# Self-attention's keys and queries leave their products turned and are moved to their heads inside SBUF

## What is computed

```python
nq = _rms(x @ w_cq, g_qnorm)                                   # latent, 96 wide
q_nope = (nq @ w_dq_nope).reshape(B, T, 16, 32)
q_rope = _rope((nq @ w_dq_rope).reshape(B, T, 16, 64), cos, sin)
q = concatenate([q_nope, q_rope], -1)
kw = (x @ w_wink).reshape(B, T, 16, 96)                        # window keys
kw = concatenate([kw[..., :32], _rope(kw[..., 32:], cos, sin)], -1)
a1 = _attn(q, k1, v1, causal=True)      # k1 from a 32 wide latent
a2 = _attn(q, ks, vs, causal=False)     # 64 selected tokens
a3 = _attn(q, kw, vw, causal=True)
out = (g0 * a1 + g1 * a2 + g2 * a3) @ w_proj
# _rope: x1 * c - x2 * s, x1 * s + x2 * c on the two halves (32 each) of the 64
```

## Time and profile before

| | us |
|---|---|
| median of 3 runs | 1769.17 (1767.9 to 1771.75) |
| the profiled execution | 1767.97 |
| its span in the trace | 1766.3 |
| PE busy | 1711.8 (97%) |
| DVE busy | 1193.7 (68%) |
| POOL busy | 1038.8 (59%) |
| ACT busy | 877.4 (50%) |

### The profile page before, as it was taken

The page is one execution under the profiler, slowest core; times in us unless marked ns, Lnnn a source line. Parts: engine busy times, 40 slices in busy tenths (PEclk is TensorE's granted clock), DMA queues, the critical chain, the costliest instruction groups (busy, mean ns, idle before and its releaser), DMA issues.

```text
span 1766.3 us, 33699 instructions
## 1 busy us (share of the span) xinstructions
PE 1711.8 (97%) x11512; PEld 1341.5 (76%) x11512; DVE 1193.7 (68%) x3890; ACT 877.4 (50%) x2824; POOL 1038.8 (59%) x1451
## 2 busy tenths in 40 slices
PE   7899999999999999999999789999999999999998
PEld 4676675766766767767657568999999999999997
DVE  4668767767777777687677568565756575657557
ACT  1675856846947848668579552222222222222221
POOL 2455655745736746657557476664856485648553
PEclk9899999999999999999999999999999999999999
DMA  5000000000000000000000110101010101010001
GB/s 179 7 2 8 7 8 7 1 8 7 2 8 7 2 8 8 1 14 2 8 1 2 49 49 25 48 1 48 1 48 1 48 1 49 1 48 1 1 1 48
DMA packets 24667, 33.89 MB, mean 19 GB/s; under 512 B 5104, under 2 KB 20976, under 8 KB 24368
## 3 DMA queue, kind: packets, MB, share of 16 engines
q1 hardware_dynamic: 24496, 31.73, 5.5%
HBM read 29.62 MB, written 2.10 MB: 18 GB/s over the span
## 4 chain that ended last, share of the span: by engine, by line
PE 84%; ACT 7%; DVE 4%; issue 3%; POOL 1%; SPq 0%; DMA 0%; DVEq 0%; POOLq 0%; ACTq 0%
PE ps_S L1423 26%; PE ps_Y L2220 20%; PE ps_H L2220 19%; ACT pr L854 5%; PE ps_O L1423 5%; PE ps_T L1655 5%; PE ps_X L1423 2%; PE ps_T L1489 2%; PE ps_X L1489 2%; PE ps_T L1773 1%; PE ps_S L1773 1%; ACT pr L908 1%; DVE h_hi L2183 1%; DVE sm L1334 0%; ACT rot L737 0%
## 5 line engine op out<-in xcount | busy, mean ns | idle before, releaser
L2054 ACT ACTIVATE h_sb<-ps_H,b_sb 128x512 f32<-128x512 f32 x256 | 176.7, 690 | 506.4 <-PE ps_H L2220 479.8
L2008 POOL TENSOR_TENSOR h_lo<-h_sb,h_hi 128x512 fp32r<-128x512 f32 x256 | 363.4, 1448 | 108.8 <-DVE h_hi L2183 108.8
L645 POOL TENSOR_TENSOR pr<-pr,rden 128x128 f32<-128x128 f32 (+2 forms) x768 | 308.0, 437 | 103.8 <-DVE rden L1215 103.8
L2183 DVE CAST h_hi<-h_sb 128x512 fp32r<-128x512 f32 x256 | 240.2, 956 | 129.7 <-ACT h_sb L2054 129.6
L854 ACT ACTIVATE pr<-sm,nmx 128x128 f32<-128x128 f32 (+2 forms) x768 | 311.7, 412 | 24.5 <-DVE nmx L1226 24.5
L2220 PE MATMUL ps_Y<-w_hi,h_lo 128*128 128x256 f32 x1024 | 286.5, 280 | 0.0
L2220 PE MATMUL ps_Y<-w_hi,h_hi 128*128 128x256 f32 x1024 | 286.5, 280 | 0.0
L2220 PE MATMUL ps_Y<-w_lo,h_hi 128*128 128x256 f32 x1024 | 286.4, 280 | 0.0
L680 POOL TENSOR_TENSOR pr<-pr,rden 128x256 f32<-128x256 f32 x256 | 151.4, 614 | 156.1 <-DVE rden L1215 156.1
L1226 DVE CUSTOM_DVE_ANT_0 sm<-ps_S,cmask 128x128 f32<-128x128 f32 (+2 forms) x768 | 192.8, 308 | 40.5 <-PE ps_S L1423 24.7
L2220 PE MATMUL ps_H<-x_hi,w_hi 128*128 128x512 f32 x512 | 200.4, 391 | 0.0
(11 more groups left out here) (241 smaller groups left out, 3284.3 us busy)
## 6 DMA issues: line engine op xcount, KB each, us to landing
w_raw<-in_W SPq DMA_DIRECT2D x16, 1024.0 KB, 6.2
xin<-in_x SPq DMA_DIRECT2D x8, 256.0 KB, 3.3
cin<-in_ctx SPq DMA_DIRECT2D x8, 256.0 KB, 2.6
w_kw<-in_wink SPq DMA_DIRECT2D x2, 768.0 KB, 6.6
w_ks<-in_selk SPq DMA_DIRECT2D x2, 768.0 KB, 9.9
out<-x SPq DMA_DIRECT2D x3, 512.0 KB, 2.9
b_sb<-in_b SPq DMA_DIRECT2D x1, 1024.0 KB, 4.7
w_qd<-in_dq SPq DMA_DIRECT2D x1, 576.0 KB, 4.8
```

Of the source, the lines that this page charges most:

```text
L645: last = pool.tensor_tensor(p_, p_, rden[:, h % 2, n:n + 1].to_broadcast([P, width]), ALU.mult)
L2008: pool.tensor_tensor(h_lo[:, s % 2, ht, :], h_sb[:, ht % 4, :], h_hi[:, s % 2, ht, :].bitcast(F32), ALU.subtract).then_inc(lo_sb.sem, 1)
L2054: ins = act.activation(h_sb[:, ht % 4, :], pst[plan.bank(f)][:, :], ACT.Relu, bias=b1[:, 2 * i + s // NCH, ht:ht + 1])
L2183: dve.tensor_copy(h_hi[:, s % 2, ht, :], h_sb[:, ht % 4, :]).then_inc(hi_sb.sem, 1)
```

## The change

Keys and queries are now computed with the weights held and all 256 tokens moving (`turned_product`), so that features are in the partitions from the start. A unit is now one half of the heads for all 256 tokens. The columns of `dq` and `wink` are put in another order on the host (`STRIP_HEADS`), so that a part of a unit is a tile of 128 partitions (four strips of 32 features, one head each) x 512 (two heads x 256 tokens); these tiles are `pieces`, in the memory of `rot`. Cosine and sine are loaded once more in turned form (`cs_turned`, 128 x 512, 256 KB), as a fifteenth first weight. Rotation, sums and evacuations work on `pieces`. The 16 groups of transposes per row and the 16 copies out of PSUM are gone for these four units; the selected keys are turned as before. Instead `moves` on SyncE issues transfers from `pieces` to `kT` and `qT`, one for each part and strip: 12, 12, 16 and 16 for the units, 56 a row and 448 in all, each 32 partitions x 2 heads x 256 tokens (64 KB). POOL and ACT wait for the transfers of unit u-2 where they waited for its last turn, and PE waits for all four units before head 0.

```diff
+STRIP_HEADS = [4 * j + b for b in range(4) for j in range(4)]
+STRIPS = P // HD
...
-    for n, name in enumerate((
-            ("kwT", 0, 0), ("kwT", 0, 1), ("kwT", 0, 2), "latT", ("kwT", 0, 3),
-            *(("kwT", 1, g) for g in range(4)), *(("qT", t, g) for t in range(NT) for g in range(4)),
-            ("ksT", 0), ("ksT", 1))):
+    for n, name in enumerate(("latT", ("ksT", 0), ("ksT", 1))):
...
+        cs_turned = sb("cs_turned", [P, 2, T])
...
+        pieces = rot[:, :, :, :].rearrange("p u h d -> p u (h d)").rearrange("p u (s n) -> p u s n", s=4)
...
+        moved = [Signal(sem(f"moved_{u}"), 16 * STRIPS * (3 if u < 2 else 4)) for u in range(4)]
...
+        def landed(eng, u, i):
+
+            eng.wait_ge(moved[u].sem, moved[u].at(i + 1, 0))
...
-        N_FIRST, N_MID, N_LATE = 14, 5, 11
+        N_FIRST, N_MID, N_LATE = 15, 5, 11
...
+            load(cs_turned[:, :, :], w["cs_turned"])
...
+            def move(i, u, part):
+
+                kind, half = UNITS[u]
+                for j in range(STRIPS):
+                    dst = slice(HD * part, HD * part + HD)
+                    heads_ = slice(4 * j + 2 * half, 4 * j + 2 * half + 2)
+                    to = kT[dst, heads_, KEEP:KEEP + T] if kind == "kw" else qT[dst, heads_, :]
+                    sp.dma_start(to, pieces[HD * j:HD * j + HD, u % 2, part, :].rearrange("p (h t) -> p h t", h=2)
+                                 ).then_inc(moved[u].sem, 16)
+
+            def moves(i):
+
+                for u in range(4):
+                    sp.wait_ge(rope_out.sem, rope_out.at(i, 2 * u + 1))
+                    move(i, u, 1)
+                    sp.wait_ge(rope_out.sem, rope_out.at(i, 2 * u + 2))
+                    move(i, u, 2)
+                    sp.wait_ge(plan.free_sem(unit_fill(u, "n")), plan.after(unit_fill(u, "n"), i))
+                    move(i, u, 0)
+                    if u >= 2:
+                        sp.wait_ge(plan.free_sem(unit_fill(u, "c")), plan.after(unit_fill(u, "c"), i))
+                        move(i, u, 3)
+
             def turn(i, load_x):
...
                 load_ctx(i, 1)
+                moves(i + 1)
...
                 def rope_sums(u):
                     rows_, n = unit_rows(u)
                     if u >= 2:
-
-                        pool.wait_ge(plan.full_sem(last_turn(u - 2)), plan.after(last_turn(u - 2), i))
...
+                        landed(pool, u - 2, i)
...
                     if u >= 2:
-
-                        act.wait_ge(plan.full_sem(last_turn(u - 2)), plan.after(last_turn(u - 2), i))
-                    ins = act.copy(rows_[:, :, 0:HD], ps(f)[0:n, :].rearrange("p (h d) -> p h d", h=NH))
+                        landed(act, u - 2, i)
+                    if u < 4:
+                        ins = act.copy(pieces[:, u % 2, 0, :], ps(f)[:, :])
...
-                    evacuate(i, f, rot[:, t, :, QK:P], ps(f)[:, :].rearrange("p (h d) -> p h d", h=NH))
+                    evacuate(i, f, pieces[:, t, 3, :], ps(f)[:, :])
...
+                def turned_product(name, weights, moving):
+
+                    pe.wait_ge(plan.free_sem(name), plan.before(name, i))
+                    for b in range(2):
+                        block_ = slice(P * (2 * name[1] + b), P * (2 * name[1] + b) + P)
+                        for c, (w_, x_) in enumerate(zip(weights, moving)):
+                            last = mm(ps(name)[:, T * b:T * b + T], w_[:, block_], x_, c == 0, c == len(weights) - 1)
+                    last.then_inc(plan.full_sem(name), 1)
+
                 def keys(t, s):
-                    product(i, ("kw", t, "nab"[s]), P, HW, tok(xT, t), [w_kw[:, c, s, :] for c in range(NC)])
+                    turned_product(("kw", t, "nab"[s]), [w_kw[:, c, s, :] for c in range(NC)],
+                                   [xT[:, c, :] for c in range(NC)])
...
                 def queries(t, s):
-                    product(i, ("q", t, "nabc"[s]), P, HW, [latT[0:QL, 0, P * t:P * t + P]], [w_q[:, s, :]])
+                    turned_product(("q", t, "nabc"[s]), [w_q[:, s, :]], [latT[0:QL, 0, :]])
...
                 if h == 0:
 
-                    pe.wait_ge(plan.free_sem(("qT", 1, 3)), plan.after(("qT", 1, 3), i))
-                    pe.wait_ge(plan.free_sem(("qT", 1, 2)), plan.after(("qT", 1, 2), i))
+                    for u in range(4):
+                        landed(pe, u, i)
```

More of the change, by code:

```diff
@@ L401, in attention_stage, with split4, strip_part @@
         cmp2 = sb("cmp2", [P, NT, T])
+        pieces = rot[:, :, :, :].rearrange("p u h d -> p u (h d)").rearrange("p u (s n) -> p u s n", s=4)
+        def split4(row):
+            return row.rearrange("p (b t n) -> p b t n", b=2, t=NT)
+        def strip_part(k):
+            if k < 3:
+                at = NT * T + k * (HW // PR_SLOTS)
+                return pr[:, :, at:at + HW // PR_SLOTS].rearrange("p (b t) n -> p b t n", b=2)
+            return split4(rt3[:, :])
         def rot_part(k, n):
@@ L567, in _ @@
             load_ctx(0, 0)
+            moves(0)
             sp.wait_ge(plan.full_sem("xsel"), plan.after("xsel", 0))
@@ L1427, in _ @@
             stage = pr[0:HD, :, :].rearrange("p a b -> p (a b)")
-            for h in range(NH):
-                last = mm(pst["S0"][0:QL, HD * h:HD * h + HD], stage[:, QL * h:QL * h + QL],
+            for n, h in enumerate(STRIP_HEADS):
+                last = mm(pst["S0"][0:QL, HD * n:HD * n + HD], stage[:, QL * h:QL * h + QL],
                           stage[:, NH * QL + HD * h:NH * QL + HD * h + HD])
@@ L1467, in front, with turn_selected @@
             def front(i):
-                def turn_rows(u, groups):
-                    kind, t = UNITS[u]
-                    rows_, n = unit_rows(u)
-                    if kind == "ks":
-                        pe.wait_ge(sel_nope.sem, sel_nope.at(i, 1))
-                    else:
-                        pe.wait_ge(plan.free_sem(unit_fill(u, "n")), plan.after(unit_fill(u, "n"), i))
-                    if kind == "q":
-                        pe.wait_ge(plan.free_sem(unit_fill(u, "c")), plan.after(unit_fill(u, "c"), i))
-                    pe.wait_ge(rope_out.sem, rope_out.at(i, 2 * u + 2))
-                    width = P if kind == "q" else QK
-                    per = 8 if kind == "ks" else 4
-                    for g in groups:
-                        f = ("ksT", g) if kind == "ks" else (kind + "T", t, g)
+                def turn_selected():
+                    rows_, n = unit_rows(4)
+                    pe.wait_ge(sel_nope.sem, sel_nope.at(i, 1))
+                    pe.wait_ge(rope_out.sem, rope_out.at(i, 10))
+                    for g in range(2):
+                        f = ("ksT", g)
@@ L1485, in turn_rows @@
                         pe.wait_ge(plan.free_sem(f), plan.before(f, i))
-                        if kind == "ks":
-                            pe.sem_inc(s_pass, 1)
-                        for k in range(per):
-                            last = pe.transpose(ps(f)[0:width, n * k:n * k + n], rows_[:, per * g + k, 0:width],
+                        pe.sem_inc(s_pass, 1)
+                        for k in range(8):
+                            last = pe.transpose(ps(f)[0:QK, n * k:n * k + n], rows_[:, 8 * g + k, 0:QK],
```

90 lines of the change are left out of this document (29 added, 61 removed).

## The result

The changed kernel takes 1754.36 us (median of five runs, 1749.06 to 1758.62) against 1769.17 for the kernel before, a ratio of 0.9914 with a 95% interval of 0.9889 to 0.9939. It is faster by 0.9%, 26 us slower than the forecast of 1728, and outside the range of 1711 to 1748. The profiled execution took 1749.06 us, span 1747.0, against 1767.97 and 1766.3 before. Measured again beside some of the experiments, the changed kernel took 1759.10 us (1755.80 to 1764.37, six runs). The runs of each kernel scatter: those five lie 9.6 us apart, six of the changed kernel 8.6, and eleven of the kernel before, beside these six, 10.1.

A forecast was written before the change was run, and what follows sets the result against it. TensorE was taken to bound the kernel. Seven rows -37.1, row 0 -5.4 and the start +1.7 gave -40.8 us: profiled 1767.97 to 1727.2, plus 1.2 to the median, 1728.4, predicted as 1728, range 1711 to 1748.

The forecast's parts named there:

- a rule on transfers: Skill's bandwidth rule for the transfers inside SBUF: 0.95 us for 64 KB, against 0.50 us between loads in the trace.
- Removed on PE: In each row, 16 groups of four transposes at 0.44 us leave TensorE: 7.0 us a row.
- New waits: In each row, three waits of TensorE for DVE and ACT grow: 1.7 us a row together, bounds 0 and 3.5.
- Wait (a): Queries of unit 3, at 406.20 us, wait for the bank that ACT's copy frees: 0.5 us a row.
- Wait (b): The product at 412.83 us and its partner wait for banks read by DVE's rotations: 0.6 us a row.
- Wait (c): The scores pair at 419.45 us waits for an ACT copy of 418.33: 0.6 us a row.
- Row 0: First row, without cover: head 0 at 61.0 us instead of 66.45, set by 32 transfers at 0.50 us; gain 5.4 us.
- the slow rival: SyncE's queue becomes the bound: at 0.95 us a transfer, one after another, +34 us, 1803; chance 0.13.
- The start: Before the first matmul, the added 256 KB table lands later than the other first weights: costs 1.7 us, bounds 0.6 and 2.5.
- Transfers hidden in rows 1 to 7: Before head 0 in rows 1 to 7, the transfers have at least 11 us of slack and cost nothing.
- Turned products at nothing: Keys and queries products in the new form cost nothing extra; bounds 0 and 0.09 us for each of 14 products a row.
- waits take the place of the transposes: Rival: in each row the removed transposes covered the DVE and ACT loop, 3.5 us come back: 1743; chance 0.19.

The follow-up runs named there:

- the kernel with the clock held: The changed kernel plus, in each row, 14 dead transposes where TensorE waits and two small dead matmuls before head 0; 1738.77 us.
- the kernel with the moved product: The kernel with the clock held, with the first product of latent values moved from a later step in place of 8 fillers; 1740.29 us.

## Why the prediction was wrong

**The clock, which no term held.** The whole sum stood on groups at clock 1.00, since the earlier trace rows show 1.00, and I never asked what kept it there. Held by fillers, the changed kernel takes 1738.77 us, inside the range; bare, 1754.36 and 1759.10. The falls cost 15.6 and 20.3 us. That is 0.59 of the first miss, 26.4 us, and 0.65 of the 31.1 by the second measurement, and it is shown: fillers in the idles bring it back without taking away any work or transfer; the same fillers elsewhere do not. The Trainium skill, "TensorE: Matmul & The Clock Gate", section "A second HAM failure mode: psum-queue depth-cycling", describes small idles between groups of matmuls, frequent enough that the clock goes to and fro between its two levels. This trace agrees, on fp32 work: five idles of 0.23 to 0.92 us in 30 us, none of them long, and the clock falls there in some rows and not in others. The prediction weighed a rule on transfers against the trace and should have weighed this one.

**Removed on PE, 7.0 us a row: right.** The line turns only 64-column transposes, 128 of them.

**New waits, 1.7 us a row: too small, 2.6.** A row without a fall gains 4.2 to 4.6 us, 4.4 in the middle, so 7.0 - 4.4 = 2.6 came back. Wait (a), behind ACT's copy, was priced at 0.5 and is 0.52. Wait (b), behind DVE's rotations, was priced at 0.6; it is 0.23 as idle and 2.33 - 1.89 = 0.44 more inside the group at 283.62: 0.67. Wait (c), the scores pair behind ACT's copy, was priced at 0.6 and is 0.92. Not priced were a first queries group stretched from 1.89 to 2.23 (at 271.05), and 0.11 more before head 0. Together 0.52 + 0.67 + 0.92 + 0.34 + 0.11 = 2.56, or 2.4 less the old idle of 0.17 that is gone. Seven rows of 0.9 are the 6 us of this step.

**Row 0, gain of 5.4: wrong, 0.4 came.** The mechanism was named, the transfer was mis-sized. Head 0 came at 67.78 in place of 62.7, 5.1 us late: 66.45 + 1.7 - 67.78 = 0.4 is left of the gain. The working said that the gain is 0 at t = 0.65; t is 0.64 to 0.69. I had taken the 0.50 us of loads, with 0.42 and 1.0 as its ends, and the sum used the 0.50. At that price the transfers behind unit 2's first sum set head 0; at the true one all 56 do, without a gap from the first. What the spacing in the earlier trace rows could not show is the price of an issue whose source is in SBUF; the same 590 ns with half the bytes says that it is a price per issue. The 0.95 us of the slow rival didn't come either, so nor did its 1803. Without transfers head 0 came at 62.97, where the working had 60.2 + 1.7 = 61.9: the path through the engines was 1.1 us too short as well, hidden beneath.

**The start, +1.7: right.** 11.48 us against 9.77; with the table behind the first weights it is 9.85.

**Transfers hidden in rows 1 to 7: right, nearly.** PE waits for no transfer there. With the clock held they cost 0.2 us a row, through 0.3 us more before head 0.

**Turned products at nothing: right.** A turned keys or queries group of eight passes takes 1.89 us where the old one took 1.88. **Sums unchanged: right,** 1266 and 1268 ns in the median of the two sums, where those before took 1269 and 1270.

Put together, from 1728.4: row 0, 5.1; rows, 6.1; that gives 1739.6, and the kernel with the clock held measures 1738.8. Then 15.6 to 20.3 for the clock. Of the rivals, "waits take the place of the transposes" had the right place and side, but counted only the time of the waits; a wait here costs more than it lasts: 2.6 us a row of waits brought another 2 to 3 us a row of lower clock.

What stays open: which rows are hit in a run, and how much of the difference between the changed kernel's 15.6 to 20.3 us of falls and the 7 us of the one without transfers is from the longer wait before head 0, and how much from traffic. That half the bytes went with 7.7 us less leaves a share of the traffic possible; that 448 transfers beside the old order cost nothing, and beside the filled one no clock, suggests that it would need the idles for it. Why the clock falls in row 0 of every kernel wasn't tried.

## What to carry to other kernels

- Before work is taken off an engine that sets the time, ask what its rows were covering: list the waits that lie beneath, and the clock that the engine's steadiness was granted. A stretch at clock 1.00 is no promise for the same stretch with work taken out of it.
- Where such idles stay, fill them: a dead transpose is nearly free there, and a real product shortens the row by 0.5 us more, as long as no new wait comes in its place. Compare the periods and the windows of the clock row by row; a mean clock that goes from 0.993 to 0.983 hides a few rows that lose 5 us each.
- Many small transfers inside SBUF cost one issue each, 32 KB as much as 64 KB, so their count sets the price where nothing covers them; and on a computing engine's queue the issues stand in the way of its own work.

## What the runs showed of the hardware

- In rows where TensorE idled five times for 0.2 to 0.9 us, its granted clock fell to its lower level in two to seven of seven rows, at about the same places and in different rows from run to run; a row that was hit lost 1.6 to 5.1 us. With 0.50, 0.17 and 0.39 us of idle in the same stretch no row after row 0 was hit.
- One fall began while TensorE was busy, some 8 us behind the last idle (408 to 414 us of the kernel with the moved product, clock 0.72).
- A transfer inside SBUF of 32 or 64 KB over 32 partitions holds SyncE's queue for 0.59 us (0.64 to 0.69 with the step to the next) and lands 1.9 to 2.0 us after issue in the median; ScalarE needs 0.62 us for one. A load of cin from outside takes 0.37.
- 448 transfers of 60 KB beside unchanged work moved the time by nothing that can be measured (a ratio of 0.9996).
